# A fused decoder on one core: the last encoder layer's third norm moved one tile on, and a top-32 selection written as a difference of exponentials

## What is computed

```
scores = Q K^T / sqrt(32)                  # 4 heads, 112 x 375
topv, topi = top_k(scores, 32)
attn = zeros.at[topi].set(softmax(topv))   # mean over the heads
c_t = (attn_mean @ V) * mask
```

## Time and profile before

| | us |
|---|---|
| median of 3 runs | 2401.41 (2398.43 to 2401.81) |
| the profiled execution | 2396.02 |
| its span | 2394.2 |
| TensorE busy | 2103.9 (88%) |
| VectorE busy | 1514.4 (63%) |
| GpSimd busy | 810.4 (34%) |
| ScalarE busy | 711.3 (30%) |
| mean granted clock of TensorE | 0.894 |

### The profile page before, as it was taken

The page is one execution under the profiler, slowest core; times in us unless marked ns, Lnnn a source line. Parts: engine busy times, 40 slices in busy tenths (PEclk is TensorE's granted clock), DMA queues, the critical chain, the costliest instruction groups (busy, mean ns, idle before and its releaser), DMA issues.

```text
span 2394.2 us, 37754 instructions
## 1 busy us (share of the span) xinstructions
PE 2103.9 (88%) x15300; PEld 1469.6 (61%) x15300; DVE 1514.4 (63%) x3047; ACT 711.3 (30%) x1407; POOL 810.4 (34%) x726
## 2 busy tenths in 40 slices
PE   6988979999999978999999999988567767879986
PEld 2334337777766656888888888776445555446632
DVE  7998955566333325556556555666398998737556
ACT  6445324333311222232223222222142222121132
POOL 3242448966500014444444444432270000013101
PEclk9768689999899989999999999999766675889998
DMA  5222173222010027101001000100231110310001
GB/s 154 70 75 90 57 161 92 60 67 71 7 53 1 1 94 173 34 1 69 1 2 51 19 1 1 52 1 1 71 100 29 30 30 25 87 49 1 0 0 31
DMA packets 67181, 114.47 MB, mean 48 GB/s; under 512 B 34153, under 2 KB 58722, under 8 KB 65794
## 3 DMA queue, kind: packets, MB, share of 16 engines
q1 hardware_dynamic: 67010, 112.07, 16.3%
HBM read 91.56 MB, written 33.34 MB: 52 GB/s over the span
## 4 chain that ended last, share of the span: by engine, by line
PE 64%; DVE 25%; POOL 6%; issue 3%; ACT 2%; DMA 0%; SPq 0%; DVEq 0%; POOLq 0%; ACTq 0%
PE PS L1534 8%; PE PS L1550 8%; PE PS L1280 5%; PE PS L1258 4%; DVE top L2334 4%; DVE w_s L2343 4%; PE PS L2214 2%; DVE ln_st L270 2%; PE PS L2204 2%; PE PS L1447 2%; PE PS L1461 2%; PE PS L2143 2%; PE PS L892 2%; PE PS L879 2%; PE PS L409 2%
## 5 line engine op out<-in xcount | busy, mean ns | idle before, releaser
L289 POOL TENSOR_SCALAR ln_ve<-ln_mv 128x2 f32<-128x2 f32 (+1 forms) x87 | 20.0, 230 | 1195.5 <-DVE ln_mv L273 1195.4
L1807 POOL TENSOR_TENSOR q_x<-q_f,cols 128x2048 f32<-128x2048 f32 x56 | 217.9, 3911 | 9.7 <-ACT q_f L1638 8.0
L1762 DVE TENSOR_TENSOR p_x<-PS,cols 128x1024 f32<-128x1024 f32 x112 | 129.3, 1218 | 134.3 <-PE PS L1496 134.3
L1089 DVE TENSOR_REDUCE XD<-PS 112x2 f32<-112x750 f32 x128 | 120.0, 940 | 96.0 <-PE PS L879 95.6
L457 PE MATMUL PS<-bc_parts,ident 96*128 96x448 bf16 x256 | 106.0, 518 | 41.2 <-DVE st_h L691 28.0
L1048 ACT ACTIVATE e_t<-PS 125x672 f32<-125x672 f32 x128 | 93.5, 730 | 154.8 <-PE PS L892 154.8
L1337 DVE SCALAR_TENSOR_TENSOR XA<-PS,gate_w,XA 112x256 f32<-112x256 f32 x128 | 56.0, 480 | 125.6 <-PE PS L1280 125.6
L2096 PE MATMUL PS<-dg,e_p 112*125 112x112 f32 x384 | 80.1, 400 | 61.7 <-ACT dg L2292 61.7
L1625 ACT ACTIVATE wb<-PS,cols 128x256 f32<-128x256 f32 x224 | 90.8, 472 | 142.8 <-PE PS L1534 142.8
L879 PE MATMUL PS<-enc_w,q_s 32*112 32x375 f32 x512 | 130.6, 535 | 1.7 <-DVE XD L1089 1.7
L892 PE MATMUL PS<-q_s,enc_w 32*125 32x112 f32 x1536 | 121.9, 289 | 2.6 <-ACT e_t L1048 2.6
(11 more groups left out here) (366 smaller groups left out, 4710.6 us busy)
## 6 DMA issues: line engine op xcount, KB each, us to landing
k_full_scratch<-k_scratch SPq DMA_DIRECT2D x112, 112.0 KB, 2.9
v_all_scratch<-v_st SPq DMA_DIRECT2D x16, 750.0 KB
v_t<-v_all_scratch SPq DMA_DIRECT2D x16, 750.0 KB
t_ring<-k_full_scratch SPq DMA_DIRECT2D x8, 784.0 KB, 12.4
enc_w<-in_enc_w SPq DMA_DIRECT2D x2, 3072.0 KB, 11.2
wc<-in_enc_w SPq DMA_DIRECT2D x2, 3072.0 KB, 12.2
k_all_scratch<-k_st SPq DMA_DIRECT2D x16, 375.0 KB
enc_w<-k_all_scratch SPq DMA_DIRECT2D x64, 93.8 KB, 3.5
```

The source lines that it names most:

```text
L1089: dve.tensor_reduce(nm_w[0:T, g % 4, 64 * half + 16:64 * half + 49:32], PS[0:T, 2 * half:2 * half + 2, 0:S2], AX.X, ALU.max, negate=True). ...
L1762: last = dve.tensor_tensor(p_x[:, m, :, :, :], ps[1][:, m * P:(m + 1) * P].rearrange("p (h i) -> p h i", i=16).unsqueeze(2) .to_broadcast( ...
L1807: last = pool.tensor_tensor(q_x[:, c, :, :].rearrange("p t (h i) -> p t h i", i=16), q_f[:, k % 2, c, :].rearrange("p (t i) -> p t i", i=1 ...
```

## The change

Two places.

1. Encoder, last layer. `second_norm` ends with the affine. `last_stats` (the residual's add and the third norm's statistics) stands at the end of VectorE's step, behind the next tile's `first_norm`, and `last_apply` (the two L282 instructions, then `n2_done`) in the step after that, between `v_z` and `p_x`. TensorE turns the result between the two halves of `feed_in`; ScalarE copies it between the two halves of the relu.
2. Selection. The replaced copy `w_s` gets a place for each of the four heads. When the fourth turn is done (`x_sel`), ScalarE takes Exp of `w_s` in place (0 where a value was replaced) and Exp of the 32 kept values with their sum (`rest_and_sum`, then `x_rest`). GpSimd subtracts: `e_p - w_s` leaves the 32 kept ones (`x_cut`), and forms the weights' factor by a power of -1 and the mask. L2353, L2356 and L2357 are gone. VectorE waits for `x_rest` and `x_cut` of the same head of the batch before. The orders are new: PE makes `attend(b)`, keys of b+2, scores of b+2 for heads 0 and 1, `gather(b)`, scores for heads 2 and 3, `values`; ScalarE makes the weights of b-1 behind Exp of heads 0 and 1 of b, and `copy_values` one batch later. GpSimd's input norm is cut into one row or one affine half per head, each behind a subtract. The masks are bfloat16. `at_t` moves into `wa`.

In the diff a line of "..." marks what is left out.

```diff
         dg = sb("dg", [T, 2, XH, T], pool=s4a)
-        at_t = sb("at_t", [JR, 2, JC, T], pool=s4a)
+        minus = sb("minus", [T, XH], pool=s4a)
+        at_t = wa[0:JR, :, :].rearrange("p k n -> p (k n)")[:, 0:2 * JC * T].rearrange("p (z j t) -> p z j t", z=2, j=JC)
...
@@ -660,7 +661,7 @@
             dve.wait_ge(const_loaded, 80)
-            for k in range(3):
+            for k in range(4):
...
@@ -1576,7 +1578,7 @@
                     scores(k - 1)
-                if 0 <= k - 3 < STEPS and k != STEPS + 1:
+                if 0 <= k - 3 < LAST_0 or k == STEPS + 2:
...
@@ -1590,10 +1592,10 @@
                     turn_residuals()
-                if k == STEPS + 1:
-                    turn_second(k - 3)
...
                     feed_in(k - 2, 0)
+                    if LAST_0 <= k - 3:
+                        turn_second(k - 3)
...
@@ -1615,6 +1617,15 @@
                         .then_inc(xg0_copied, 1)
+            def copy_last(i):
+                r = i % ROUNDS
+                act.wait_ge(ez_ready, i + 1)
+                for c in range(KC):
+                    last = act.copy(
+                        XF[:, c, :].rearrange("p (b t) -> p t b", b=B)[:, 16 * r:16 * r + 16, :],
+                        ps[3][:, c * RT:(c + 1) * RT].rearrange("p (t b) -> p t b", b=B))
+                last.then_inc(ez_copied, 1)
...
@@ -1673,6 +1679,8 @@
                     relu(k - 2, 0)
+                    if LAST_0 <= k - 3:
+                        copy_last(k - 3)
...
@@ -1708,12 +1716,20 @@
                 link(normed(x))
-                if layer < LAYERS - 1:
-                    affine(layer, x, "g2", "be2", n2_done)
-                else:
-                    affine(layer, x, "g2", "be2", None)
-                    link(dve.tensor_tensor(x, x, xg0[:, 2 * r:2 * r + 2, :], ALU.add))
-                    normed(x).then_inc(n2_done, 1)
+                affine(layer, x, "g2", "be2", n2_done if layer < LAYERS - 1 else None)
+            def last_stats(i):
+                r = i % ROUNDS
+                x = xg[:, 2 * r:2 * r + 2, :]
+                link(dve.tensor_tensor(x, x, xg0[:, 2 * r:2 * r + 2, :], ALU.add))
+                return norm_stats(dve, link, [x[:, g, :] for g in range(2)], P)
+            def last_apply(i, k):
+                r = i % ROUNDS
+                for g in range(2):
+                    x = xg[:, 2 * r + g, :]
+                    last = norm_apply(dve, k, g, x, x, P)
+                last.then_inc(n2_done, 1)
...
@@ -1756,6 +1773,8 @@
                     last.then_inc(ev_copied, 1)
+                if LAST_0 <= k - 3 < STEPS:
+                    last_apply(k - 3, waiting)
...
@@ -1771,6 +1790,9 @@
                     second_norm(k - 2)
+                if LAST_0 <= k - 2:
+                    waiting = last_stats(k - 2)
+            last_apply(STEPS - 1, waiting)
...
@@ -1816,9 +1838,9 @@
                     norm_root(pool, link, 2, P)
-                    if k - 2 >= STEPS - ROUNDS:
-                        norm_root(pool, link, 2, P)
                 if 0 <= k - 1 < STEPS and k != STEPS:
+                    norm_root(pool, link, 2, P)
+                if LAST_0 <= k - 2 < STEPS:
...
@@ -2016,9 +2038,10 @@
             for b in range(B):
-                if 1 <= b < B - 1:
-                    uses.append(("k", b + 1))
-                uses += [("at", b), ("m1", b)]
+                uses.append(("at", b))
+                if b + 2 < B:
+                    uses.append(("k", b + 2))
+                uses.append(("m1", b))
...
@@ -2049,13 +2072,14 @@
-        def topk_masks(pool):
+        def topk_masks(pool, link):
...
             pool.tensor_scalar(mskb[:, :], msk8[:, :], -1.0, -FAR, ALU.add, ALU.mult).then_inc(e_prep, 1)
-            pool.tensor_scalar(tmk[:, :], tmk8[:, :], 1.0, None, ALU.mult).then_inc(e_prep, 1)
+            pool.tensor_scalar(tmk[:, :], tmk8[:, :], 1.0 / XH, None, ALU.mult).then_inc(e_prep, 1)
+            link(pool.memset(minus[:, :], -1.0))
...
                               start=True, stop=False)
-                    pe.matmul(ps[h][0:T, 0:S2], ident[r, 32 * h + b:32 * h + b + 1].to_broadcast([32, T]), mskb[r, :],
+                    pe.matmul(ps[h][0:T, 0:S2], ident16[r, b:b + 1].to_broadcast([32, T]), mskb[r, :],
...
@@ -2120,21 +2144,23 @@
             pe.wait_ge(e_prep, 3)
-            scores(0)
+            scores(0, range(XH))
...
                 turn_rows(j)
-            for b in range(B):
-                if b + 1 < B:
-                    if b >= 1:
-                        topk_keys(pe, b + 1)
-                    scores(b + 1)
-                    attend(b)
-                    gather(b)
-                    if b % QB == QB - 1:
-                        values(b // QB)
+            scores(1, range(XH))
+            for b in range(B - 1):
+                attend(b)
+                if b + 2 < B:
+                    topk_keys(pe, b + 2)
+                    scores(b + 2, (0, 1))
+                gather(b)
+                if b + 2 < B:
+                    scores(b + 2, (2, 3))
+                if b % QB == QB - 1:
+                    values(b // QB)
...
@@ -2256,11 +2282,26 @@
                 act.copy(m1[0:CR[1], 1, b * T:(b + 1) * T], bank[0:CR[1], T:2 * T]).then_inc(m_used, 1)
-                if b % QB == QB - 1:
-                    q = b // QB
-                    for c in range(KC):
-                        act.copy(c_t[:, c, q * QT:(q + 1) * QT], m_bank(act, "ct", 2 * q + c)[:, 0:QT])\
-                            .then_inc(m_used, 1)
+            def copy_values(q):
+                for c in range(KC):
+                    act.copy(c_t[:, c, q * QT:(q + 1) * QT], m_bank(act, "ct", 2 * q + c)[:, 0:QT])\
+                        .then_inc(m_used, 1)
+            def rest_and_sum(b, h):
+                act.wait_ge(x_sel, XH * b + h + 1)
+                bias = neg_m[:, h:h + 1]
+                act.activation(w_s[:, h, :], w_s[:, h, :], ACT.Exp, bias=bias)
+                tops = top8[:, h, :, :].rearrange("t r v -> t (r v)")
+                act.activation(tops, tops, ACT.Exp, bias=bias, accum_out=e_sum[:, b % 2, h:h + 1])\
+                    .then_inc(x_rest, 1)
+            def weights(b):
+                act.wait_ge(x_rs, b + 1)
+                for h in range(XH):
+                    last = act.activation(dg[:, b % 2, h, :], ident[0:T, 0:T], ACT.Copy,
+                                          scale=e_rs[:, b % 2, h:h + 1])
+                last.then_inc(x_dg, 1)
...
-                        copy_attention(b - 1)
-                        copy_context(b - 1)
-                        if b + 1 < B:
-                            copy_keys(b + 1)
-                act.wait_ge(x_rs, b + 1)
-                for h in range(XH):
-                    last = act.activation(dg[:, b % 2, h, :], ident[0:T, 0:T], ACT.Copy,
-                                          scale=e_rs[:, b % 2, h:h + 1])
-                last.then_inc(x_dg, 1)
+                    if h == 1:
+                        if b == 0:
+                            copy_keys(1)
+                            for j in range(B // 2):
+                                copy_rows(j)
+                        else:
+                            weights(b - 1)
+                            copy_attention(b - 1)
+                            if b + 1 < B:
+                                copy_keys(b + 1)
+                        rest_and_sum(b, 0)
+                        rest_and_sum(b, 1)
+                        if b >= 1:
+                            copy_context(b - 1)
+                    elif h == 3:
+                        if b >= 1 and b % QB == 0:
+                            copy_values(b // QB - 1)
+                        rest_and_sum(b, 2)
+                        rest_and_sum(b, 3)
+            weights(B - 1)
...
             copy_context(B - 1)
+            copy_values(NQ - 1)
...
                                 dve.wait_ge(x_s_ready, n + 1)
+                                if b >= 1:
+                                    dve.wait_ge(x_rest, n - 3)
...
                                 link.after(cut[a])
-                            s = ps[h][0:T, 0:S2] if turn == 0 else w_s[:, a, :]
-                            found[a] = link.mark(dve.max(top8[:, a, turn, :], s))
+                            s = ps[h][0:T, 0:S2] if turn == 0 else w_s[:, h, :]
+                            found[a] = link.mark(dve.max(top8[:, h, turn, :], s))
...
                                 link.after(found[a])
-                                found[a] = link.mark(dve.tensor_scalar(neg_m[:, h:h + 1], top8[:, a, 0, 0:1], -1.0,
+                                found[a] = link.mark(dve.tensor_scalar(neg_m[:, h:h + 1], top8[:, h, 0, 0:1], -1.0,
...
                             link.after(found[a])
-                            s = ps[h][0:T, 0:S2] if turn == 0 else w_s[:, a, :]
-                            ins = dve.match_replace(w_s[:, a, :], top8[:, a, turn, :], s, FILL)
```

(56 more changed lines are left out.)

57 lines of the change are left out of this document (24 added, 33 removed).

## The result

The changed kernel takes 2418.24 us (median, 2416.52 to 2419.03); the kernel before, in runs on the same chip, 2399.92. The ratio is 1.0074 with a 95% interval of 1.0059 to 1.0090: slower by some 18 us. The prediction said slower, 2438, with a range of 2394 to 2464; its two terms, +13 and +26, came to twice the 18 us that were measured.

A forecast was written before the change was run, and what follows sets the result against it. VectorE was taken to bound the selection, and the last layer's third norm to lengthen the encoder's steps. 2396.0 + 13 (encoder) + 26 (selection) = 2435, stated as 2438 for the median; range 2394 to 2464.

The forecast's parts named there:

- its two terms, +13 and +26: Encoder +13 us, bounds -10 and +17; selection +26 us, by the bounds of the clock -28 and +58.
- The application waits for GpSimd: Encoder's last layer: last_apply waits for GpSimd's second q_x product, so TensorE stands 4.8 us a step; 1.9 without the wait.
- The clock behind the stand: Encoder's last layer: TensorE's clock falls behind its stand, so feed_in's second half, turn and turn_probs take 2.8 us more.
- Four steps: Encoder's last layer, k = 24 to 27: steps of 35.6 us, together +21 us against 121.3 before.
- the last two rounds: Encoder's end, without q_x: first round -3.4 us; second -4.3, feed_in's first half running under tile 27's third norm.
- The turn's own price on TensorE: Encoder's last layer: the turn, now on TensorE's path between n1_done and project, adds 0.49 us a step.
- rival C: From e3's own forecast: moved turn and copy cost by their place between feed_in's halves; steps 33 us or more.
- The start: Selection: weights of batch 0 begin at about 1764.9 against 1752.90, +12 us, after row copies, subtracts and norm rows.
- The lap of the ring: Selection: the loop from one batch's weights through TensorE, ScalarE and GpSimd to the next takes 19.1 us, against VectorE's 15.9.
- The three intervals with the values: Selection: copy_values keeps ScalarE from rest_and_sum three times, 6.3 us each, 19 in all.
- rival 3: Ring links shorter, 17.4 us a batch: selection +2, encoder -10 to +10, about 2404 us; chance 0.13.
- Rival 2: Selection: TensorE stays at the upper clock level, ring 15.1 us, VectorE's 15.9 decides; 2384 us, or 2361; chance 0.10.

The follow-up runs named there:

- e5: e3 with GpSimd's bias and q_x products in the last layer's steps waiting until the application is done: 2376.59 us, ratio 0.9906.
- e3: Changed kernel with the third norm's application moved into VectorE's wait for the exponentials, ahead of GpSimd's q_x products: 2386.99 us, ratio 0.9962.
- e6: Changed kernel with 13 extra matmuls in each of TensorE's stands for the application in the last layer: 2405.18 us, ratio 1.0023.
- e1: Kernel before with only the encoder's part of the change: 2410.13 us, ratio 1.0059.
- e8: Changed kernel with GpSimd's norm rows behind the scaling of the weights and the row copies spread over the first batches: 2403.91 us, ratio 1.0024.
- e2: Kernel before with only the selection's part of the change: 2399.61 us, ratio 1.0011.
- e10: Changed kernel with 17 extra matmuls in each of TensorE's 16 waits for the selection's weights: 2384.32 us, ratio 0.9946.
- e4: Changed kernel with 24 extra matmuls in each of TensorE's stands for the application in the last layer: 2417.63 us, ratio 1.0085.
- e9: Changed kernel without the fourth MATCH_REPLACE8 of each head, so the weights hold 24 of the 32 largest: 2414.31 us, ratio 1.0069.
- e11: e5 with e8's moves and with ScalarE's copy of the values moved last in the batch: 2357.84 us, ratio 0.9823.

## Why the prediction was right in direction and twice too high

**The application waits for GpSimd: right.** Predicted a stand of 4.8 us, measured 6.41. The cause is as it was put, from the one pair in the earlier trace rows, and e5 shows it. The size was 1.6 short because of a step left out: `last_stats` gives GpSimd a root (1533.77 to 1534.78 above) that stands ahead of the bias and of `q_x`. So the products start 1535.99 - 1532.07 = 3.92 us behind the turn of `x1`, where I had 1.97 from the earlier trace rows: 2 us later. Of these, 0.3 came back because the application ended 0.47 us behind the second product and not 0.81. I had counted what `last_stats` adds to VectorE and not what it adds to GpSimd's list. The Trainium skill (SBUF — State Buffer, Who interferes with whom) says that whichever engine begins first holds the shared ports for its whole instruction; e3 and e5 agree with it, 4.99 and 0.73 us.

**The clock behind the stand: right**, 2.8 a step by estimate, 2.5 by e6. The step's sum has a slip: its terms make 35.5, not 35.6.

**Four steps: +21 predicted, +25.8 measured; the last two rounds -7.7 predicted, -12.2 measured.** Both terms were short by some 4.5 and cancelled: +13 predicted, 13.5 by the cut, 12.5 by e1's medians. The sum was right, by luck. In the steps the missing part is the longer stand. In the last two rounds, between the score copy at 1675.79 and the first MAX8, the first of my two terms held (the turn of `x1` comes 3.84 us behind the score copy for 7.38, -3.5 for -3.4) and the second was too small: from the turn of tile 26's third norm to the end of `feed_in` the kernel before took 11.2 us (1.12 for the turn, 1.53 of waiting, 8.70 in the earlier trace rows). The changed kernel takes 4.0:

```profile
1717.38 0.67 PE L1431 MATMUL PS<-ident,XA 128*128 128x128 f32 x4 [1.40 <-DVE XA L283]
1717.89 3.62 PE L1536 MATMUL PS<-wc 128*128 128x256 f32 x16
```

That is -7.2 for -4.3: the wait is gone, and the granted clock is 1.00 in both rows. Some 1.5 us more are spread over the rest of the two rounds. The turn's own price on TensorE, 0.49 in the prediction, is borne out: e5's steps, with turn and copy in their new place, are 27.89 us for the 27.43 of the layers before, and rival C's larger price is not there.

**The start, +12: right**, 31.8 us for 31.5; e8 takes 8.6 of it back, so it was row copies and norm rows.

**The lap of the ring, 19.1 predicted, 17.39 measured: the step that failed.** Link by link from the rows above, in us:

| link | predicted | measured |
|---|---|---|
| weights and hand-over | 1.36 | 1.37 |
| attention | 5.2 | 5.14 |
| keys, copy and hand-overs | 3.22 | 2.70 |
| scores of two heads | 1.4 | 0.98 |
| gather | 2.1 | 1.67 |
| copy of the context | 0.45 | 0.29 |
| two Exps | 1.1 | 0.93 |
| the two rests | 1.5 | 1.60 |
| GpSimd | 2.75 | 2.71 |

Of the 1.7 us that the lap is shorter than predicted, 1.4 are in the three TensorE links behind the attention. I had taken each of them as a mixture of the upper and the lower level, since the earlier trace rows show a gather at 0.50. In this lap the granted clock is 0.50 in the attention, 0.76 in the keys, and 1.00 in the scores and the gather (the keys take 2.13 us; scores and gather, 0.89 and 1.64, have the upper level's figures of the earlier trace rows). What I had missed is the order: the kernel before has the gather directly behind the attention, at 1.61 or 2.90 us; the new order puts keys and scores between them, and it is the keys that still pay for the lower level. The gather took 1.64 us in each of the 14 batches with keys ahead of it, and 2.90, at 0.50, in the one batch whose attention also took 5.35 us and which has none left to make:

```profile
2060.23 2.90 PE L2131 MATMUL PS<-wa,ctx_k 125*128 125x112 f32 x12 [0.57 <-ACT wa L2278]
```

Fourteen laps of 1.7 us make 24 us. The three intervals with the values went the other way: 24.7 us above calm ones, 19 predicted (the values ran at 7.04, 3.86 and 7.23 us; I had taken 4.5 for each). Weights 0 to 15 came to 291.5, not 310.

So the selection went as rival 3 had it (17.4 a batch, +2, "it only moves the wait"), and the encoder as the forecast had it. With rival 3's +2 in place of +26 my own sum is 2396.0 + 13 + 2 = 2411, or 2414 with the 3 us that I laid on top for the median; measured 2418.2. e2's medians, +2 with an interval of 0.5 to 5, bear that term out; the cut of the changed kernel alone has +7.6 in it (12.3 - 4.7).

**Rival 2, the upper level throughout: not this kernel, but one edit away.** It gave 15.1 for the ring and VectorE as the bound; e10 comes near that case, with a lap of 14.4 in places and weights 0 to 15 in 262.0 us. Rival 2's 256 does not follow from the terms that it names.

Still open: why the same selection takes 285.6 to 291.5 us in executions that differ only ahead of it. The values of four batches take 3.86 us in some places and 7.0 to 7.2 in others. The first of them took 3.86 in e2, e3, e5 and e6, whose interval there is 24.2 us, and 7.04 in the changed kernel, e4 and e9, with 28.5 or 28.6: 4.3 of the 6 us. The old selection has the same: 7.20, 3.83 and 7.20 in the kernel before, 3.83, 7.20 and 3.83 in e1. So it is again the level of the clock at that moment; what decides it there was not tried.

## What to carry to other kernels

When work moves to another engine's shadow, read that engine's list and ports there: an operation of 0.73 us took 3.4 to 5.0 because a GpSimd product ran beside it, and making GpSimd wait 0.9 us for it was worth 10 us in all. When a stage turns into a ring through several engines, price TensorE's links at the level that its wait in the ring leaves it, link by link, and ask whether the wait can be filled: seventeen matmuls of no use a batch were worth 31 to 34 us. A loss of 18 us can hide a gain: with its order mended the same change was 41 us faster than the kernel before (e11), so look for the order before giving the change up.
